# The token lists of six experts: indirect stores of (row, weight) pairs in place of one-hot products on TensorE

## The reference

```
scores = (xn @ Wg.T).T                      # 8 experts x 8192 tokens
top_vals, token_idx = top_k(scores, 1024)   # each expert picks 1024 tokens
token_w = softmax(top_vals)
xg = xn[token_idx]
h = silu(xg @ W1[e].T) * (xg @ W3[e].T)     # 1024 hidden columns
y = (h @ W2[e].T) * token_w
out.at[token_idx].add(y)
```

## Time and profile before

| | |
|---|---|
| three runs | 1980.72, 1975.03, 1978.11 us; median 1978.11 |
| the profiled execution | 1978.15 us, of which the span is 1976.4 |
| TensorE busy | 1939.4 us, 98% |
| VectorE busy | 1161.4 us, 59% |
| ScalarE busy | 648.4 us, 33% |
| POOL busy | 595.2 us, 30% |

### The profile page before, as it was taken

How to read it: one execution, slowest core, us unless ns; L and a number is a source line. 1 busy time by engine, 2 the same in 40 slices (tenths; PEclk the granted TensorE clock), 3 DMA queues, 4 the chain that set the end, 5 groups by cost and what they waited for, 6 DMA issues and landing times.

```text
span 1976.4 us, 39583 instructions
## 1 busy us (share of the span) xinstructions
PE 1939.4 (98%) x16755; PEld 1571.7 (80%) x16755; DVE 1161.4 (59%) x1661; ACT 648.4 (33%) x953; POOL 595.2 (30%) x410
## 2 busy tenths in 40 slices
PE   8999999999999999999999999999999999999998
PEld 7777777777778887778788888888888888888886
DVE  7787887876888877776444345443543453434321
ACT  4333333333344343323333332332332323323321
POOL 2445445445354444541211220212112202121111
PEclk9999999999999999999999999999999999999999
DMA  7466565663323332234433442532433435324311
GB/s 203 131 174 188 169 175 155 174 158 121 87 81 87 87 87 82 66 109 158 97 118 86 88 114 76 132 84 60 129 85 83 104 89 127 82 60 135 64 22 22
DMA packets 172720, 214.65 MB, mean 109 GB/s; under 512 B 31776, under 2 KB 105888, under 8 KB 172576
## 3 DMA queue, kind: packets, MB, share of 16 engines
q1 hardware_dynamic: 146096, 154.92, 27.8%
q0 software_dynamic: 14336, 33.56, 9.6%
q10 hardware_dynamic: 12144, 24.12, 3.4%
HBM read 128.13 MB, written 51.38 MB: 91 GB/s over the span
## 4 chain that ended last, share of the span: by engine, by line
PE 51%; DVE 1%; SPq 1%; ACT 0%; issue 0%; DMA 0%; POOL 0%; POOLq 0%
PE ps_e L59 17%; PE ps_e L60 17%; PE ps_e L61 17%; SPq L199 1%; PE ps_e L159 1%; DMA raw<-in_w 0%; ACT w_hi L1775 0%; DVE xn L1896 0%; DVE w_lo L1890 0%; DVE hm L1922 0%; DVE xgt_lo L1901 0%; DVE x_f L147 0%; DVE hot_more L147 0%; DVE hot_v L137 0%; POOL out_rows L1739 0%
## 5 line engine op out<-in xcount | busy, mean ns | idle before, releaser
L59 PE MATMUL ps_e<-xgt_hi,w_hi 128*128 128x512 f32 x1024 | 401.4, 392 | 0.0
L60 PE MATMUL ps_e<-xgt_lo,w_hi 128*128 128x512 f32 x1024 | 398.8, 389 | 0.0
L61 PE MATMUL ps_e<-xgt_hi,w_lo 128*128 128x512 f32 x1024 | 398.7, 389 | 0.0
L1922 DVE TENSOR_TENSOR hm<-ps_e,silu 128x512 f32<-128x512 f32 x128 | 88.4, 691 | 456.4 <-PE ps_e L61 455.7
L1739 POOL DMA_INDIRECT out_rows<-x_res,idx x64 | 100.6, 1572 | 429.7 <-ACT x_res L1807 415.9
L61 PEld LDWEIGHTS ps_e<-xgt_hi,w_lo 128*128 128x128 f32 x1024 | 192.3, 188 | 40.0
L59 PEld LDWEIGHTS ps_e<-xgt_hi,w_hi 128*128 128x128 f32 x1024 | 192.3, 188 | 39.1 <-DVE xgt_lo L1901 0.2
L60 PEld LDWEIGHTS ps_e<-xgt_lo,w_hi 128*128 128x128 f32 x1024 | 192.4, 188 | 38.7
L188 POOL DMA_INDIRECT x_in<-xn_rows,idx x64 | 77.7, 1213 | 476.6 <-DVE idx L180 304.0
L59 PE MATMUL ps<-xt_hi,wqk_hi 128*128 128x512 f32 x512 | 206.2, 403 | 2.7 <-POOL xt_lo L542 1.5
L1795 ACT ACTIVATE h_hi<-hm 128x512 fp32r<-128x512 f32 x128 | 80.9, 632 | 383.9 <-DVE hm L1922 383.9
(11 more groups left out here) (199 smaller groups left out, 3400.9 us busy)
## 6 DMA issues: line engine op xcount, KB each, us to landing
x_f<-in_w SPq DMA_DIRECT2D x48, 512.0 KB, 3.9
raw<-in_w SPq DMA_DIRECT2D x48, 512.0 KB, 3.7
x_res<-in_x SPq DMA_DIRECT2D x16, 1024.0 KB, 5.7
xn<-x_in SPq DMA_DIRECT2D x256, 64.0 KB, 2.0
pt<-pn_sb SPq DMA_DIRECT2D x248, 64.0 KB
out_rows<-x_res ACTq DMA_DIRECT2D x15, 1024.0 KB, 4.2
xn_rows<-xt_plain SPq DMA_DIRECT2D x8, 1024.0 KB, 4.4
x_in<-xn_rows SPq DMA_DIRECT2D x28, 256.0 KB, 4.5
```

Source lines behind the costliest of these rows:

```text
L59: nc.tensor.matmul(out, w_hi, x_hi, start=start, stop=False)
L60: nc.tensor.matmul(out, w_hi, x_lo, start=False, stop=False)
L61: return nc.tensor.matmul(out, w_lo, x_hi, start=False, stop=stop)
L1922: v.tensor_tensor(hm[:, m % 2, :], ps[:, 2 * (m % 2) + 1, :], silu[:, m % 2, :], ALU.mult).then_inc(hm_ready, 1)
```

## The change

Lists 0 and 1 are made as before. For lists 2 to 7, VectorE works out once, in expert 0, for all tokens and the six experts a pair (token number, weight) and the row of a table in memory where it belongs (`list_pairs`): row place in a block of the expert for a chosen token, row 1024 + token number of the same block for one that is not chosen. POOL stores the pairs with indirect DMAs, 64 for each expert (128 pairs of 8 bytes in each), in expert e for list e + 2: 16 ahead of the gather of half q + 2 and 48 behind it (`store_pairs`). Behind every fourth it waits until the batch before the last has landed. SP loads the first 1024 rows of the block as the list (`load_list`, behind the weight loads of expert e for list e + 1, ahead of the spread of half q + 1). It waits for all stores of that list and for the scatters of all experts up to e - 1, which read the buffer until then. Gathers wait for this load in place of `idx_ready`. The one-hot work of lists 2 to 7 on VectorE and TensorE is left out, the list's buffer holds pairs, and POOL's loop over experts is written out.

```
@@ -40,6 +40,9 @@
...
 NT = N // P
+LATER = E - 2
+LIST_ROWS = N // E + N
+BATCH = 4
 NS = CAP // P
...
@@ -94,8 +97,9 @@
...
         self.got, self.idx_f = sb("got", [P, 5, NS]), sb("idx_f", [P, NS])
-        self.idx = [sb(f"idx_{i}", [P, NS], U32) for i in range(2)]
-        self.weight = [sb(f"weight_{i}", [P, NS]) for i in range(2)]
+        self.list_in_use = [sb(f"list_{i}", [P, NS, 2]) for i in range(2)]
+        self.idx = [t[:, :, :].bitcast(U32)[:, :, 0] for t in self.list_in_use]
+        self.weight = [t[:, :, 1] for t in self.list_in_use]
...
@@ -177,8 +184,8 @@
...
     dve.wait_ge(k.list_step, STEPS * e + 3)
-    v.tensor_copy(k.idx[par][:, :], k.idx_f[:, :]).then_inc(k.idx_ready, 1)
-    v.tensor_tensor(k.weight[par][:, :], k.got[:, 2, :], k.got[:, 4, :], ALU.add).then_inc(k.list_step, 1)
+    v.tensor_copy(k.idx[par], k.idx_f[:, :]).then_inc(k.idx_ready, 1)
+    v.tensor_tensor(k.weight[par], k.got[:, 2, :], k.got[:, 4, :], ALU.add).then_inc(k.list_step, 1)
@@ -187,7 +194,7 @@
...
             out=k.x_in[:, t, :], out_offset=None, in_=xn_rows,
-            in_offset=bass.IndirectOffsetOnAxis(ap=k.idx[par][:, tile0 + t:tile0 + t + 1], axis=0)).then_inc(k.xg_in, 16)
+            in_offset=bass.IndirectOffsetOnAxis(ap=k.list_in_use[par][:, :, :].bitcast(U32)[:, tile0 + t, 0:1], axis=0)).then_inc(k.xg_in, 16)
@@ -201,6 +208,48 @@
 SPREAD = 16 * NQ * NQ
...
+def list_pairs(nc, dve, k, pairs, dest, spare):
...
+    v = nc.vector
+    shape = [P, LATER, NT]
+    tok, at, off = spare[:, 0:NT], spare[:, NT:NT + LATER * NT], spare[:, NT + LATER * NT:NT + 2 * LATER * NT]
+    past = spare[:, NT + 2 * LATER * NT:2 * NT + 2 * LATER * NT]
+    at, off = (t.rearrange("p (e n) -> p e n", e=LATER) for t in (at, off))
+    slots = [s[:, 2:E, :] for s in (k.slot_a, k.slot_b)]
+    parts = [k.wgt_parts[:, 2:E, :, j] for j in range(3)]
+    dve.wait_ge(k.hot_mm, 2 * GROUPS)
+    v.tensor_scalar(tok, k.iota_t[:, :], float(P), k.iota_p[:, 0:1], ALU.mult, ALU.add).then_inc(k.pair_step, 1)
+    v.scalar_tensor_tensor(at, slots[0], float(P), slots[1], ALU.mult, ALU.add).then_inc(k.pair_step, 1)
+    v.tensor_tensor(pairs[:, :, :, 1], parts[0], parts[1], ALU.add).then_inc(k.pair_step, 1)
+    dve.wait_ge(k.pair_step, 2)
+    v.tensor_copy(pairs.bitcast(U32)[:, :, :, 0], tok.unsqueeze(1).to_broadcast(shape)).then_inc(k.pair_step, 1)
+    v.tensor_scalar(past, tok, float(CAP - N), None, ALU.add).then_inc(k.pair_step, 1)
+    dve.wait_ge(k.pair_step, 5)
+    v.scalar_tensor_tensor(off, at, float(N), past.unsqueeze(1).to_broadcast(shape), ALU.is_ge, ALU.mult).then_inc(k.pair_step, 1)
+    v.tensor_tensor(pairs[:, :, :, 1], pairs[:, :, :, 1], parts[2], ALU.add).then_inc(k.pair_step, 1)
+    dve.wait_ge(k.pair_step, 7)
+    for e in range(LATER):
+        i = v.scalar_tensor_tensor(at[:, e, :], at[:, e, :], float(LIST_ROWS * e), off[:, e, :], ALU.add, ALU.add)
+    i.then_inc(k.pair_step, 1)
+    dve.wait_ge(k.pair_step, 8)
+    v.tensor_copy(dest, at).then_inc(k.pairs_ready, 1)
...
+def store_pairs(nc, pool, k, list_rows, pairs, dest, e, tiles):
...
+    pool.wait_ge(k.pairs_ready, 1)
+    pool.nop(nofuse=True)
+    for n in tiles:
+        batch = (NT * (e - 2) + n) // BATCH
+        stored = k.list_stored[batch % 2]
+        if n % BATCH == 0 and batch >= 2:
+            pool.wait_ge(stored, 16 * BATCH * (batch // 2))
+            pool.nop(nofuse=True)
+        nc.gpsimd.indirect_dma_start(
+            out=list_rows, out_offset=bass.IndirectOffsetOnAxis(ap=dest[:, e - 2, n:n + 1], axis=0),
+            in_=pairs[:, e - 2, n, :], in_offset=None).then_inc(stored, 16)
@@ -1663,6 +1712,8 @@
...
         hot_sets = lists.hot_sets + [hot_more[:, i, :, :] for i in range(2)]
+        pairs = lists.x_f[:, 0:2, :].rearrange("p a b -> p (a b)")[:, 0:2 * LATER * NT].rearrange("p (e n v) -> p e n v", e=LATER, v=2)
+        dest = lists.wgt[:, 0:LATER, :].bitcast(U32)
         silu, hm = sb("silu", [P, 2, T]), sb("hm", [P, 2, T])
...
@@ -1704,6 +1755,12 @@
...
+            def load_list(e):
+                for stored in lists.list_stored:
+                    sp.wait_ge(stored, 16 * NT // 2 * (e - 1))
+                sp.wait_ge(scattered, 16 * TT * HALVES * (e - 1))
+                sp.dma_start(lists.list_in_use[e % 2][:, :, :], d["lists"][e - 2, :, :, :]).then_inc(lists.list_in, 16)
...
             def expert(e, last=False):
...
@@ -1711,6 +1768,8 @@
...
                     load_unit(e, u)
+                if 1 <= e < E - 1:
+                    load_list(e + 1)
                 if e >= 1:
...
@@ -1725,7 +1784,10 @@
...
-                pool.wait_ge(lists.idx_ready, e_idx)
+                if e_idx <= 2:
+                    pool.wait_ge(lists.idx_ready, e_idx)
+                else:
+                    pool.wait_ge(lists.list_in, 16 * (e_idx - 2))
                 pool.wait_ge(lists.xs_in, SPREAD * q)
...
@@ -1737,27 +1799,33 @@
...
                     nc.gpsimd.indirect_dma_start(
-                        out=d["out"], out_offset=bass.IndirectOffsetOnAxis(ap=lists.idx[par][:, tile0 + t:tile0 + t + 1], axis=0),
+                        out=d["out"], out_offset=bass.IndirectOffsetOnAxis(ap=lists.list_in_use[par][:, :, :].bitcast(U32)[:, tile0 + t, 0:1], axis=0),
                         in_=y[:, t, :], in_offset=None, compute_op=ALU.add).then_inc(scattered, 16)
...
-            def expert(e, par, first=False, last=False):
+            def store(e, tiles):
+                if e < E:
+                    store_pairs(nc, pool, lists, d["list_rows"], pairs, dest, e, tiles)
...
+            def expert(e, par, last=False):
                 q = HALVES * e
                 gather_half(q + 1, par, TT, e + 1)
-                if not first:
+                if e >= 1:
                     scatter(q - 1, 1 - par, TT)
+                    store(e + 2, range(NT // 4))
                 if not last:
                     gather_half(q + 2, 1 - par, 0, e + 2)
-                scatter(q, par, 0)
...
-            expert(0, 0, first=True)
-            expert(1, 1)
-            with pool.Fori(1, E // 2 - 1) as i:
-                expert(2 * i, 0)
-                expert(2 * i + 1, 1)
-            expert(E - 2, 0)
-            expert(E - 1, 1, last=True)
+                if e == 0:
+                    store(2, range(NT // 4))
+                    scatter(q, par, 0)
+                    store(2, range(NT // 4, NT))
+                else:
+                    store(e + 2, range(NT // 4, NT))
+                    scatter(q, par, 0)
...
+            for e in range(E):
+                expert(e, e % 2, last=e == E - 1)
             scatter(HALVES * E - 1, 1, TT)
...
@@ -1864,16 +1932,16 @@
...
-            def expert(e, last=False):
+            def expert(e, first=False, last=False):
                 q = HALVES * e
-                up(q, e, True, next_list=not last)
-                down(q, e, True, next_list=not last)
+                up(q, e, True, next_list=first)
+                down(q, e, True, next_list=first)
                 up(q + 1, e, False)
...
                 nc.tensor.matmul(ps[:, LISTS, 0:P], lists.ident[:, :], lists.ident[:, :], start=True, stop=True)
-            expert(0)
+            expert(0, first=True)
             with pe.Fori(1, E - 1) as e:
...
@@ -1926,16 +1994,14 @@
...
-            def expert(e, par, first=False, last=False, second_next=True):
+            def expert(e, first=False, last=False):
                 q = HALVES * e
-                half(q, FIRST_SPLITS if first else [(e, FM + i) for i in range(FM // 2)],
-                     lists_of=None if last else e + 1, first=first)
-                if not last:
-                    expert_list(nc, dve, lists, e + 1, 1 - par, scattered)
+                half(q, FIRST_SPLITS if first else [(e, FM + i) for i in range(FM // 2)], lists_of=1 if first else None, first=first)
+                if first:
+                    expert_list(nc, dve, lists, 1, 1)
                 xgt_lo_part(q + 1)
-                if second_next:
-                    places_one_hot(nc, dve, lists, e + 2)
-                    weights_one_hot(nc, dve, lists, e + 2)
+                if first:
+                    list_pairs(nc, dve, lists, pairs, dest, hot_more[:, :, :, :].rearrange("p s t b -> p (s t b)").bitcast(F32))
                 half(q + 1, [] if last else [(e + 1, i) for i in range(FM)], last=last)
...
@@ -1964,6 +2027,8 @@
...
         xn = nc.dram_tensor("xn_rows", [N, C], F32, kind="Internal").ap()
+        list_rows = nc.dram_tensor("list_rows", [LATER * LIST_ROWS, 2], F32, kind="Internal").ap()
+        list_blocks = list_rows.rearrange("(e r) v -> e r v", e=LATER)[:, 0:CAP, :].rearrange("e (a b) v -> e b a v", b=P)
         gate = nc.dram_tensor("gate_rows", [4, P, T], F32, kind="Internal").ap()
...
@@ -1971,7 +2036,7 @@
...
         attention_block(nc, d, lists)
-        expert_block(nc, {"xn": xn, "out": out, "w13": w13, "w2": w2}, lists)
```

(15 more changed lines are left out.)

## The result

The changed kernel took **2328.92 us** (median of 4 runs, 2300.3 to 2335.97) against 1978.82 for the kernel before (4 runs, 1975.03 to 1980.72): ratio **1.1715** (95% interval 1.1668 to 1.1762). The ratio and its interval go by the fast runs alone, so they are not the quotient of the two medians. The forecast was 351 us too low, and its range and all its rivals missed the time.

What follows compares the result with a forecast made beforehand. TensorE, busy for 98% of the span, was taken as the bound: 1978.15 - 11.8 for removed matmuls + 11.1 for one stall of the first list = 1977.5, rounded to 1978 us, with an eight-in-ten range of 1967 to 2003.

Steps and rivals of the forecast that it cites:

- The removed matmuls: TensorE, first halves: 64 matmuls fewer for each of lists 2 to 7, 1.97 us each, -11.8 us in all.
- list_pairs: VectorE, once in expert 0: making the pairs takes 5.4 us from 958.7, ready at 964.1, covered for TensorE.
- The price of the store: POOL: each indirect store step costs 1.25 us like the gather, with 1.1 as lower and 1.89 as upper end.
- the third rival: POOL's store costs the scatter's 1.89 us, so POOL sets the pace from expert 1 on; about 2110 us, chance 0.12.
- Interference only from the VectorE operation running at the start: POOL's stores: only a VectorE operation already running delays one; 7 us in all before scatter(0) in the first list.
- GpSimd would be kept out for whole operations: Rival 4: VectorE's operations block POOL for their whole length; stall grows by 7 to 10, 1985 to 1988, chance within second rival's.
- The stall of the first list: Expert 1: late list 2 stores delay spread(3) and VectorE's transpose, so TensorE stalls near unit 7, +11.1 us once.
- No transfer is that close to its limit: 0: DMA: 8,192 more packets per list take at most 31 us of each engine out of 131, costing 0.
- the second rival: POOL's store step costs 1.35 to 1.6 us, also by interference or landings; stall 18 to 34, 1984 to 2000, chance 0.22.
- unless something else becomes late enough to hold TensorE up: Whole kernel: time leaving TensorE is gained, VectorE's is not; POOL's new work matters only by when POOL comes to things.

Runs made afterwards that it cites:

- a_pitch: The changed kernel with its table's rows 512 bytes apart instead of dense 8-byte rows; 1982.97 us, one run.
- light sessions: Sessions of runs in which kernels with POOL's row of 64 stores per list show no slow TensorE matmuls; the changed kernel took 2003.42 us there.
- heavy sessions: Sessions in which kernels with POOL's row of 64 transfers per list show TensorE matmuls 2 to 3 us apart; the changed kernel took 2328.92 and 2306.25 us.
- c_gather8: The kernel before, one-hot lists kept, plus 384 POOL gathers of 128 rows of 8 bytes; 2341.76 us, ratio 1.1824 (1986.77 in an earlier single run).
- v_order: The changed kernel with rows 64 B apart, list 2's last 16 stores behind gather(3) and scatter(1), load_list behind the spread; 1972.86 us, later 2381.15.

## Why the prediction was wrong

Step by step:
- The removed matmuls: right. An expert of a_pitch takes 130.56, twice 65.28; in the changed kernel itself every half that had 67.33 crawls, so it can't be read there.
- list_pairs: 3.95 us for 5.4 (the 0.1 for each of four drains had no row, and the trace shows at most 0.04 between two operations), and begun 5.4 us later than forecast. The price of the store: 1.27 for 1.25, equal to the gather's of the earlier trace rows. Right, and the third rival's 1.89 fell.
- Interference only from the VectorE operation running at the start: in the changed kernel VectorE had little to do beside the stores, so a_pitch is the test. There the first store began at 967.50 (964.1 forecast) and gather(3) at 1060.33 (1058.6). Of the 92.8 us between, 64 steps of 1.27 and the scatter's 7.5 leave some 4 for interference, where the sum had 7. So the mechanism fits, but the date came out well by luck: a start that was late by 3.4 and an interference priced some 3 too high. That GpSimd would be kept out for whole operations, as a reading of the Trainium skill (GPSIMD Engine Reference, Key points) could have it, would have put that 7 to 10 us later.
- The stall of the first list: right where nothing else happened: 9.3 in a_pitch for 11.1, total 1982.97 against 1978 forecast (and 1981.51 for the kernel before beside it).
- "No transfer is that close to its limit: 0": mis-sized. With dense 8-byte rows landings get longer in the light sessions, 55.2 us of waits on POOL, and the stall is 30.5 in place of 8.4. That is the second rival's mechanism, with 22 us, and its 1984 to 2000 is about what light sessions gave with dense rows (1989.46 to 2003.42). The Trainium skill (DMA: Bandwidth & Descriptors, Specifications) gives 512 B as the least transfer for the full rate, with read-modify-write below it. No run shows such a price for 8-byte writes as such: with the rows at a pitch of 64 B POOL waited for landings for 4.0 us in all, at 512 B for 3.7, and for 55.2 only where they lay dense.
- **The step that failed**: that what leaves TensorE is gained "unless something else becomes late enough to hold TensorE up", and that POOL's transfers act on TensorE only through POOL's lateness. In the heavy sessions POOL was on time, and the stream itself slowed TensorE, to one matmul per 2.8 us, and delayed its results for the others by up to 66.4 us. The six long halves took 354 us more than they should (287.0 + 67.3), which is the whole loss, and no term of the sum stood for it. The earlier trace rows showed such transfers only in blocks of four, and I took the price of one in a block as the price of 64 in a row, for POOL and for everyone else.

What is shown: the crawl goes with the stream in time (it starts some 14 or more transfers into a stretch at full rate and ends within some 5 us of its end); it needs neither writes nor small pitch nor the table nor the removed one-hots (c_gather8); and it comes in some sessions and not in others for the same code.

What is open is the mechanism in TensorE. Late instructions would fit the idle time named "issue", the even pace and the idle DMA engines, but two things in the traces speak against them. Whole units are recorded at the normal pace and yet their results come late (unit 6 of expert 2: its 24 matmuls within 5.2 us, its hm 66.4 us after the last). And the traces hold the packets that bring instructions. On one queue a packet of 16384 B comes for about every 250 matmuls and weight loads where TensorE's program is written out. Its experts 1 to 6 are a loop, and after the first pass through it none comes: none from 1271.6 to 2188.4 in the changed kernel, where the long halves of experts 2 to 5 lie, as none from 1162.1 to 1855.4 in the kernel before. Whether TensorE's signals are late or the work behind its records, and why, the records don't say. Nor do they show whether the recording of the instructions has a part in it: every execution here was recorded. Nor is it known why a session is light or heavy, or below which rate or length of a stream the crawl doesn't come. The added transfers came with POOL's loop over experts written out, in the change and in each experiment; no kernel with that alone was run, though experts 6 and 7, written out and without stores, don't crawl.

No version beats the kernel before throughout: v_order was 1972.86 against 1978.83 in its light session, one run of each, and is 1.20 times slower in a heavy one.

## What to carry to other kernels

An engine that is at 30% and on nobody's path is not free: ask what a long unbroken stream on it does to the others, above all when the trace of before only has the operation in short blocks; the price of one says nothing on that. When one kernel's time is explained by an experiment, run the kernel itself again beside it. Here eight experiments that differed by 20 us were first read as the cure of a loss of 350 that was simply not there in those sessions. When an engine waits for the result of another, compare the start of the last instruction that makes the result with the start of its reader: here that showed what "issue" hid. Where many small rows are scattered, a pitch of 64 B is worth a trial, for one multiplication: it gave 23 us in the light sessions, but the same kernel was 83 us the slower one in the heavy ones.

## What the runs showed of the hardware

- An indirect transfer of 128 rows of 8 bytes costs POOL 0.96 + 0.30 us in either direction; the accumulating one, with rows of 2048 bytes, 1.56 + 0.30.
- At POOL's pace of 8 in 10 us a stream of them can leave TensorE at one matmul per 2.8 us, with the DMA engines 2% busy, the other engines prompt, and a granted clock of 0.5 as a consequence. TensorE's results then reach ScalarE and VectorE up to 66.4 us after the start of the last matmul, against 0.5.
- TensorE's loop of 1152 matmuls and weight loads ran from its second pass on without a packet of its instruction queue.
- Dense 8-byte rows slow other traffic in part: 300 to 331 ns for a 4096 B packet against 200 to 204; at a 64 B pitch that is gone.
